# First cross attention: one whole weighting behind the first pair of score steps, and the key and value products of the next chunk in three runs

## The chip, the cores and the metric

The kernel runs on one core of one Trainium2 chip. The metric is the device time of one execution in microseconds, as the median of several runs. The kernel before takes 999.71 us.

## The reference

A two-layer perceiver block: six sublayers update `x` (128 rows of 256 float32 values) one after the other. The change touches only the first of them, a cross attention against 12544 context rows of 256 values:

```python
    def _L0_xattn_ref(input_q, input_k, wq, wk, wv):
        N_HEADS, D_K, D_V_HEAD = 16, 64, 256 // 16
        q = (input_q @ wq).reshape(B, LQ, N_HEADS, D_K).transpose(0, 2, 1, 3)
        k = (input_k @ wk).reshape(B, LK, N_HEADS, D_K).transpose(0, 2, 1, 3)
        v = (input_k @ wv).reshape(B, LK, N_HEADS, D_V_HEAD).transpose(0, 2, 1, 3)
        attn = jnp.einsum('bhqd,bhkd->bhqk', q, k) / jnp.sqrt(jnp.float32(D_K))
        attn = jax.nn.softmax(attn, axis=-1)
        out = jnp.einsum('bhqk,bhkd->bhqd', attn, v)
        ...
    x = x + _L0_xattn_ref(_layernorm(x, axis=-1), ctx_1024, ...)
```

Self attention, a gated feed-forward layer, a second cross attention, a causal self attention and a mixture of 16 experts follow.

## The kernel before

The context is cut into a first chunk of 256 rows (chunk 0, `TAIL_TILES`) and 24 full chunks of 512 rows (chunks 1 to 24). Keys are kept in SBUF per head pair (8 pairs, `m.keys[slot]`), with two slots, one for even and one for odd chunks. PSUM has 8 banks: 0 to 3 hold scores, 4 and 5 the products of keys and values on their way to SBUF, 6 and 7 the output of the weighting.

Every engine has its own program, and the engines meet at semaphores. For one chunk of 512 rows the work is this:

- **Score steps.** There are 8 steps, each for 32 queries and 8 heads. In `scores` (L377) TensorE makes 8 products per step on 64x32 tiles of its array, which the profile shows as 16 matmuls of 512 columns, since each float32 product counts twice. Step t writes banks 0 and 1 or 2 and 3. VectorE takes the maximum (`maxima`, L598), ScalarE two exponentials (`exponentials`, L535) and signals `scores_read`, which frees the banks; VectorE transposes the probabilities (`turn_probabilities`, L617). Step t+2 can only be computed when `scores_read` of step t has come.
- **Key products.** Eight products p = 0 to 7 of the *next* chunk, 6 terms each of 128x128 weights by 512 columns (L354, the context and the weights are split in a high and a low part). ScalarE copies each to SBUF (`keep_keys`, L525) before the bank is used again.
- **Value products.** Two halves of 6 terms each (L361). VectorE transposes them out of PSUM (`turn_values`, L624), and GpSimd sets them aside in a layout with zeros (`set_aside`, L777).
- **Weighting.** `weighted` (L387) multiplies the probabilities of the *previous* chunk by its values: 16 blocks, in the profile 256 matmuls of 128 columns on 64x32 tiles. VectorE transposes the result (`turn_out`, L630), and GpSimd adds it to the sum (`add_out`).
- **Context split.** ScalarE rounds the context of the chunk after next to its high part (`split_context`, L521), and GpSimd subtracts for the low part (L743).

TensorE's order is written out by hand. Before the change `chunk` issues, per chunk, a pair of score steps and something behind it, four times: steps 2 and 3, both value halves of this chunk, the first half of the weighting; steps 4 and 5, keys 0, 1, 2; steps 6 and 7, keys 3, 4, the second half of the weighting; steps 0 and 1 of the next chunk, keys 5, 6, 7. The keys alternate between banks 4 and 5 and the value halves use one each. ScalarE's copies of keys are put between or after exponentials by `KEEP_BETWEEN` and `KEEP_AFTER`. Chunk 1 weights only the 8 blocks of chunk 0. `last_chunk` is a program of its own for chunk 24, with a smaller weighting behind each of its first four steps, and with the two value halves of its own chunk.

SyncE loads the context and issues 16 small DMAs per chunk that place the rescaling factors; GpSimd's `rescale` waits for them.

Of the kernel before, what the change touches and what calls it, by code (L numbers as in the profile page):

```python
# [12 lines left out]
P = 128  # L13
D = 256
DK = D // P
# [5 lines left out]
CHUNK_TILES = 4  # L21
# [6 lines left out]
X0_DV = D // X0_HEADS  # L28
# [319 lines left out]
def xattn0_tensor(pe, m, s, n):  # L348
# [7 lines left out]

    def value_term(slot, half, nt, i):
# [3 lines left out]
        return pe.matmul(m.bank(4 + half)[:, 0:nt * P], w[:, k, half * P:(half + 1) * P], c[:, k, 0:nt * P],  # L361
                         start=(i == 0), stop=(i == TERMS - 1))
# [29 lines left out]

    def values(slot, half, nt):
        pe.wait_ge(s["k_kept"], n("k_kept"))
        for i in range(TERMS):
            done = value_term(slot, half, nt, i)
        done.then_inc(s["v_full"], 1)
# [4 lines left out]

    def next_keys(slot, p, ahead):

        if p < 2:
            values_turned()
        if p == 0:
            pe.wait_ge(s["ctx_split"], n("ctx_split", 2))
            if ahead > 1:
                pe.sem_inc(s["raw_free"], 1)  # L410
        if p >= 2 and p != 5:
            pe.wait_ge(s["k_kept"], n("k_kept"))
        for i in range(TERMS):
            done = key_term(1 - slot, p, CHUNK_TILES, 4 + p % 2, i)
        done.then_inc(s["k_full"], 1)

    def chunk(slot, nt, nt_before, ahead):
        for t in range(0, STEPS, 2):
            if t == FIRST_KEYS:
                pe.wait_ge(s["k_kept"], n("k_kept"))  # L420
            for u in (t, t + 1):
                pe.wait_ge(s["scores_read"], n("scores_read"))
                scores(*step_after(slot, u, nt, ahead, 2))
            for half in VALUES.get(t, ()):
                values(slot, half, nt)
            for p in KEYS_AHEAD.get(t, ()):
                next_keys(slot, p, ahead)
            if nt_before:
                if t == 0:
                    pe.wait_ge(s["probs_turned"], n("probs_turned"))  # L430
                    pe.wait_ge(s["vals_ready"], n("vals_ready"))
                if t in WEIGHT_STEPS:
                    first = 2 * nt_before * WEIGHT_STEPS.index(t)
                    weighted(1 - slot, range(first, first + 2 * nt_before), 4 * nt_before - 1)
                if t == STEPS - 2:
                    pe.wait_ge(s["out_kept"], n("out_kept"))
                    pe.sem_inc(s["out_turned"], 1)

# [8 lines left out]
    def last_chunk(slot, nt, nt_before):  # L447

        for t in range(STEPS):
            after = step_after(slot, t, nt, 0, 2)  # L450
            if after:
                pe.wait_ge(s["scores_read"], n("scores_read"))
                scores(*after)
            if t < 2:
                values(slot, t, nt)
            elif t < 4:
                values_turned()
# [59 lines left out]
def xattn0_scalar(act, m, s, n):  # L517
# [4 lines left out]

    def keep_keys(slot, p, nt):
        act.wait_ge(s["k_full"], n("k_full"))
        act.copy(m.keys[slot][:, p, 0:nt * P], m.bank(4 + p % 2)[:, 0:nt * P]).then_inc(s["k_kept"], 1)  # L525

# [5 lines left out]
    def exponentials(slot, t, nt, between=None):  # L532
        act.wait_ge(s["max_ready"], n("max_ready"))
        for odd in range(2):
            i = act.activation(m.probs[t % 2][:, odd, 0:nt * P], m.ps[:, 2 * (t % 2) + odd, 0:nt * P], ACT.Exp,  # L535
                               bias=m.peak[slot][:, 1, 2 * (t // 4) + odd, t % 4:t % 4 + 1], scale=-1.0,
                               accum_out=m.totals[slot][:, 1, 2 * (t // 4) + odd, t % 4:t % 4 + 1])
            if odd == 0 and between:
                keep_keys(*between, CHUNK_TILES)
        i.then_inc(s["probs_ready"], 1)  # L540
        act.drain().then_inc(s["scores_read"], 1)  # L541

    def chunk(slot, nt, ahead, first=False):
        for t in range(2 if first else 0, STEPS):
# [7 lines left out]
            if kept:  # L552
                for p in KEEP_AFTER.get(t, ()):
                    keep_keys(keys, p, CHUNK_TILES)
            if ahead > 1 and t in SPLIT_STEPS:
                split_context(slot, SPLIT_STEPS.index(t), CHUNK_TILES)

# [6 lines left out]
    for p in range(4):  # L564
        keep_keys(0, p, TAIL_TILES)
    act.wait_ge(s["wk1"], 16)
# [5 lines left out]
    for p in range(4, 6):  # L572
        keep_keys(0, p, TAIL_TILES)
    exponentials(0, 1, TAIL_TILES)
    for p in range(6, 8):
        keep_keys(0, p, TAIL_TILES)
    for k in range(DK):
# [16 lines left out]
def xattn0_vector(dv, m, s, n):  # L594
# [26 lines left out]

    def turn_values(slot, half, nt):
        dv.wait_ge(s["v_full"], n("v_full"))
        dv.transpose(m.vals_t[slot][:, 0:4 * nt, 2 * half:2 * half + 2, :],  # L624
                     m.bank(4 + half)[:, 0:nt * P].rearrange("p (b c d) -> p b c d", c=2, d=X0_DV)
                     ).then_inc(s["v_kept"], 1)
# [6 lines left out]
    def chunk(slot, nt, order, ahead):  # L633
        for t in range(STEPS):
# [9 lines left out]
            turn_probabilities(slot, t, nt)  # L644
            for half in range(2):
                if t == TURN_STEPS[half]:
                    turn_values(slot, half, nt)

    def last_chunk(slot, nt):
        for t in range(STEPS):  # L650
            if t < STEPS - 1:
                maxima(slot, t + 1, nt)
            turn_probabilities(slot, t, nt, (LAST_HALF, STEPS - 1))
            for half in range(2):
                if t == TURN_STEPS[half]:
                    turn_values(slot, half, nt)
            if t == LAST_SUM:
# [82 lines left out]
def xattn0_pool(gp, m, s, n):  # L740
# [40 lines left out]
    def chunk(slot, nt, order, ahead):  # L781
        if order >= 1:
            rescale(1 - slot)
        set_aside(slot, nt)
        if ahead > 1:
            for k in range(DK):
                split_context(slot, k, CHUNK_TILES)
        if order >= 1:
            add_out(1 - slot, "acc_added" if ahead else "acc_whole")

    for k in range(DK):
# [990 lines left out]
```

## Time and profile before

| | us |
|---|---|
| median of 3 runs | 999.71 |
| lowest and highest | 999.46, 1000.55 |
| the profiled execution | 1000.53 |
| its span, first to last instruction | 998.6 |
| mean granted TensorE clock of the span | 0.973 of 2.4 GHz |

The span is 1.93 us shorter than the profiled execution's own time. A row of the timeline view gives the start, the duration, the engine, the line and the operation, how many instructions were merged, and in brackets how long the engine sat idle before and what ended that. PE is the matmul side of TensorE, PEld its loading of weights; a weight load and the matmul that uses it are two rows of the same line.

### The profile page before, as it was taken

What the parts mean: (1) busy time and instruction counts of PE and PEld (TensorE: products, weight loads), DVE (VectorE), ACT (ScalarE), POOL (GpSimd) and SP (SyncE); (2) the same over time, 40 slices, a digit from 0 to 9 for tenths busy, and PEclk for the clock granted to TensorE, in tenths of its full rate; (3) what the DMA queues carried; (4) which work ended last, traced back from release to release, by engine and by line L of the source; (5) the groups of instructions that cost most, each with busy time, mean ns of one, the idle gap of its engine ahead of it and who ended that gap; (6) DMA issues with size and microseconds to landing.
All of it is one profiled execution on the core that took longest, in us unless ns stands there. A gap on an engine that the chain in (4) does not pass through costs nothing.

```text
span 998.6 us, 30527 instructions
## 1 busy us (share of the span) xinstructions
PE 954.4 (96%) x13153; PEld 704.7 (71%) x13153; DVE 690.2 (69%) x871; ACT 588.8 (59%) x1404; POOL 368.8 (37%) x405
## 2 busy tenths in 40 slices
PE   6999999999999999999999999867979998989998
PEld 6666666666666666666666666556967876879998
DVE  3788888888888888888888887831035553357886
ACT  5666666666666666666666666512146662236664
POOL 2354444444444444444444443400023335013332
PEclk9999999999999999999999999986989999789999
DMA  6110000000000000000000000099058888207992
GB/s 217 30 32 15 22 22 24 24 24 24 24 24 24 24 24 24 24 24 24 24 24 24 24 4 3 3 382 358 4 197 268 278 273 305 81 1 256 335 327 101
DMA packets 78294, 97.79 MB, mean 98 GB/s; under 512 B 21584, under 2 KB 56672, under 8 KB 78176
## 3 DMA queue, kind: packets, MB, share of 16 engines
q1 hardware_dynamic: 77088, 94.40, 29.1%
q8 instruction: 103, 1.69, 0.7%
q10 hardware_dynamic: 1088, 1.57, 0.4%
q14 instruction: 15, 0.12, 0.0%
HBM read 95.42 MB, written 0.13 MB: 96 GB/s over the span
## 4 chain that ended last, share of the span: by engine, by line
PE 87%; issue 4%; DVE 3%; POOL 2%; DMA 2%; ACT 1%; SPq 1%; ACTq 0%; DVEq 0%; POOLq 0%
PE ps L354 28%; PE ps L377 17%; PE ps L387 9%; PE ps L361 7%; PE ps L1480 6%; PE ps L1088 3%; PE ps L987 3%; PE ps L1497 2%; PE ps L1501 2%; PE ps L1498 2%; PE ps L1077 1%; PE ps L1079 1%; PE ps L1078 1%; POOL m_w_lo L1463 1%; DMA m_shared_w<-in_m_sw 1%
## 5 line engine op out<-in xcount | busy, mean ns | idle before, releaser
L535 ACT ACTIVATE probs<-ps,x_peak 128x512 f32<-128x512 f32 (+1 forms) x400 | 270.2, 680 | 176.8 <-DVE x_peak L598 166.3
L598 DVE TENSOR_REDUCE x_peak<-ps 128x2 f32<-128x1024 f32 (+1 forms) x200 | 237.0, 1186 | 93.4 <-PE ps L377 93.4
L617 DVE STREAM_TRANSPOSE probsT<-probs 128x1024 f32<-128x1024 f32 (+1 forms) x200 | 242.9, 1215 | 12.9 <-ACT probs L535 12.4
L377 PE MATMUL ps<-keys,qT 64*32 64x512 f32 (+1 forms) x3200 | 195.3, 584 | 2.3 <-ACTq L541 1.6
L354 PE MATMUL ps<-ctxT_hi,wk_hi 128*128 128x512 f32 (+1 forms) x400 | 163.1, 408 | 0.8 <-ACT keys L525 0.8
L354 PE MATMUL ps<-ctxT_lo,wk_hi 128*128 128x512 f32 (+1 forms) x400 | 155.1, 388 | 0.0
L777 POOL TENSOR_SCALAR vals<-vals_t,x_side 128x512 f32<-128x512 f32 (+1 forms) x100 | 152.1, 1538 | 7.4 <-PEq L401 4.5
L354 PE MATMUL ps<-ctxT_hi,wk_lo 128*128 128x512 f32 (+1 forms) x400 | 154.3, 386 | 0.0
L354 PEld LDWEIGHTS ps<-ctxT_hi,wk_hi 128*128 128x128 f32 x400 | 75.5, 189 | 73.6 <-issue 39.8
L525 ACT COPY keys<-ps 128x512 f32<-128x512 f32 (+1 forms) x200 | 110.6, 579 | 28.2 <-PE ps L354 20.3
L743 POOL TENSOR_TENSOR ctxT_lo<-ctx_raw,ctxT_hi 128x512 fp32r<-128x512 f32 x48 | 61.8, 1287 | 135.7 <-ACT ctxT_hi L521 135.7
L377 PEld LDWEIGHTS ps<-keys,qT 64*32 64x32 f32 x3200 | 58.6, 106 | 70.0 <-issue 51.9
L387 PE MATMUL ps<-probsT,vals 64*32 64x128 f32 x6272 | 104.2, 271 | 1.4 <-DVE probsT L617 1.4
L387 PEld LDWEIGHTS ps<-probsT,vals 64*32 64x32 f32 x6272 | 90.5, 105 | 19.7 <-issue 19.5
L354 PEld LDWEIGHTS ps<-ctxT_hi,wk_lo 128*128 128x128 f32 x400 | 75.6, 189 | 15.8
L354 PEld LDWEIGHTS ps<-ctxT_lo,wk_hi 128*128 128x128 f32 x400 | 75.7, 189 | 12.3
L535 ACT ACTIVATION_READ_ACCUMULATOR probs<-ps,x_peak 128x1 f32 x400 | 79.1, 198 | 0.0
L1268 POOL TENSOR_TENSOR c1T_lo<-ctx_two,c1T_hi 128x512 fp32r<-128x512 f32 (+1 forms) x25 | 31.3, 1253 | 105.5 <-ACT c1T_hi L1149 105.5
L760 POOL TENSOR_TENSOR x_parts<-x_totals,x_shrink 128x32 f32<-128x32 f32 x24 | 6.1, 253 | 156.9 <-DMA x_shrinkT<-x_shrink 156.9
L1453 POOL TENSOR_TENSOR m_w_lo<-m_w,m_w_hi 128x1024 fp32r<-128x1024 f32 x15 | 35.5, 2364 | 75.1 <-ACT m_w_hi L1529 75.1
L1480 PE MATMUL ps<-xnT,m_w 128*128 128x128 f32 x512 | 59.9, 275 | 0.0
L1480 PEld LDWEIGHTS ps<-xnT,m_w 128*128 128x128 f32 x512 | 58.6, 192 | 0.3 <-issue 0.3
(250 smaller groups left out, 1307.7 us busy)
## 6 DMA issues: line engine op xcount, KB each, us to landing
m_w<-in_m_w SPq DMA_DIRECT2D x32, 1024.0 KB, 7.7
ctx_raw<-in_ctxT SPq DMA_DIRECT2D x24, 512.0 KB, 3.7
ctx_two<-in_ctxT SPq DMA_DIRECT2D x24, 512.0 KB, 4.0
ctx_one<-in_ctx SPq DMA_DIRECT2D x24, 512.0 KB, 5.0
x_shrinkT<-x_shrink SPq DMA_DIRECT2D x384, 1.0 KB, 1.7
f_h1T<-in_f_h1T SPq DMA_DIRECT2D x1, 4096.0 KB, 18.1
f_h2T<-in_f_h2T SPq DMA_DIRECT2D x1, 4096.0 KB, 27.9
m_shared_w<-in_m_sw SPq DMA_DIRECT2D x2, 1024.0 KB, 7.8
```

Source lines behind the costliest of these rows:

```text
L354: return pe.matmul(m.bank(bank)[:, 0:nt * P], w[:, k, p * P:(p + 1) * P], c[:, k, 0:nt * P], start=(i == 0), stop=(i == TERMS - 1))
L361: return pe.matmul(m.bank(4 + half)[:, 0:nt * P], w[:, k, half * P:(half + 1) * P], c[:, k, 0:nt * P], start=(i == 0), stop=(i == TERMS - 1))
L377: i = pe.matmul(m.ps[32 * j:32 * (j + 1), 2 * (t % 2) + odd, 0:nt * P], m.qT[rows, 4 * group + j, qs], m.keys[slot][rows, 4 * group + j, 0 ...
L387: i = pe.matmul(m.ps[32 * c:32 * (c + 1), 6 + two, 0:P], m.vals[slot][rows, b, c, :], m.probsT[slot][rows, c, b, :], start=(b == 0), stop= ...
L525: act.copy(m.keys[slot][:, p, 0:nt * P], m.bank(4 + p % 2)[:, 0:nt * P]).then_inc(s["k_kept"], 1)
L535: i = act.activation(m.probs[t % 2][:, odd, 0:nt * P], m.ps[:, 2 * (t % 2) + odd, 0:nt * P], ACT.Exp, bias=m.peak[slot][:, 1, 2 * (t // 4) ...
L598: dv.tensor_reduce(m.peak[slot][:, 1, cs, t % 4], m.ps[:, 2 * (t % 2):2 * (t % 2) + 2, 0:nt * P], AX.X, ALU.min).then_inc(s["dve" if t == ...
L617: i = dv.transpose(m.probsT[slot][:, cs, 0:4 * nt, t % 4 * 32:t % 4 * 32 + 32], m.probs[t % 2][:, :, 0:nt * P].rearrange("p c (b k) -> p c ...
L743: gp.tensor_tensor(m.c_lo[slot][:, k, 0:nt * P], m.raw[slot][:, k, 0:nt * P], m.c_hi[slot][:, k, 0:nt * P], ALU.subtract).then_inc(s["ctx_ ...
L777: t = gp.tensor_scalar(m.vals[slot][:, 0:4 * nt, cs, side * X0_DV:(side + 1) * X0_DV], m.vals_t[slot][:, 0:4 * nt, cs, :], m.side[:, side: ...
L1453: eng.tensor_tensor(m.w2_lo[c % 2][:, os, :], second_weights(m, c)[:, os, :], m.w2_hi[c % 2][:, os, :], ALU.subtract).then_inc(s[f"m_w2_lo ...
L1480: t = pe.matmul(m.bank(2 * (c % 2) + half)[:, i * P:(i + 1) * P], w1[:, k, o * P:(o + 1) * P], m.xnT[:, k, :], start=(k == 0), stop=(k == ...
```

## The change

The order of the work on TensorE in `chunk` is new. Behind steps 2 and 3 comes the whole weighting of the previous chunk. Behind steps 4 and 5 come keys 0 and 1 and value half 0 of the next chunk, behind steps 6 and 7 keys 2, 3, 4 and value half 1, behind steps 0 and 1 of the next chunk keys 5, 6, 7. So values are now made one chunk earlier than before, and `last_chunk` and its VectorE part have none left; chunk 0 makes its own values and those of chunk 1. Both value halves go through bank 4, and `KEY_BANKS` gives keys 0, 3, 6 bank 4 and the others bank 5.

The other engines follow: VectorE turns the value halves after steps 4 and 6; ScalarE copies key 2 between the two exponentials of step 6 and splits the context after steps 3 and 5 (before: 5 and 7); VectorE turns the output at step 3 (before: 7); GpSimd's order in a chunk is rescale, split, add the output, split, set the values aside (before: rescale, set aside, two splits, add).

```diff
-VALUES, KEYS_AHEAD = {0: (0, 1)}, {2: (0, 1, 2), 4: (3, 4), 6: (5, 6, 7)}
-WEIGHT_STEPS, FIRST_KEYS = (0, 4), 6
-TURN_STEPS, SPLIT_STEPS, SUM_STEP = (2, 2), (5, 7), 7
-KEEP_BETWEEN, KEEP_AFTER = {0: 5, 4: 0}, {1: (6, 7), 5: (1, 2), 6: (3,), 7: (4,)}
+KEY_BANKS = (4, 5, 5, 4, 5, 5, 4, 5)
+TURN_STEPS, SPLIT_STEPS, SUM_STEP = (4, 6), (3, 5), 3
+KEEP_BETWEEN, KEEP_AFTER = {0: 5, 4: 0, 6: 2}, {1: (6, 7), 5: (1,), 6: (3,), 7: (4,)}
...
     def chunk(slot, nt, nt_before, ahead):
...
+        two_steps(slot, 0, nt, ahead)
+        if nt_before:
+            pe.wait_ge(s["probs_turned"], n("probs_turned"))
+            pe.wait_ge(s["vals_ready"], n("vals_ready"))
+            weighted(1 - slot, range(4 * nt_before), 4 * nt_before - 1)
+            pe.wait_ge(s["k_kept"], n("k_kept", 2))
+        else:
+            for half in range(2):
+                values(slot, half, nt, 4 + half)
+        two_steps(slot, 2, nt, ahead)
+        next_context(ahead)
+        for p in range(2):
+            if not nt_before:
+                values_turned()
+            keys(1 - slot, p, False)
+        values(1 - slot, 0, CHUNK_TILES, 4)
+        if nt_before:
+            pe.wait_ge(s["out_kept"], n("out_kept"))
+            pe.sem_inc(s["out_turned"], 1)
+        two_steps(slot, 4, nt, ahead)
+        keys(1 - slot, 2, True)
+        values_turned()
+        keys(1 - slot, 3, False)
+        keys(1 - slot, 4, True)
+        values(1 - slot, 1, CHUNK_TILES, 4)
+        two_steps(slot, 6, nt, ahead)
+        keys(1 - slot, 5, True)
+        values_turned()
+        keys(1 - slot, 6, False)
+        keys(1 - slot, 7, True)
...
     def last_chunk(slot, nt, nt_before):
...
-            if t < 2:
-                values(slot, t, nt)
-            elif t < 4:
-                values_turned()
+            if t == 1:
+                pe.wait_ge(s["k_kept"], n("k_kept", 2))
...
     def chunk(slot, nt, order, ahead):
         if order >= 1:
             rescale(1 - slot)
-        set_aside(slot, nt)
+        else:
+            set_aside(slot, nt)
         if ahead > 1:
-            for k in range(DK):
-                split_context(slot, k, CHUNK_TILES)
+            split_context(slot, 0, CHUNK_TILES)
         if order >= 1:
             add_out(1 - slot, "acc_added" if ahead else "acc_whole")
+        if ahead > 1:
+            split_context(slot, 1, CHUNK_TILES)
+        if ahead:
+            set_aside(1 - slot, CHUNK_TILES)
```

In the new code `two_steps(slot, t, ...)` waits for `scores_read` and computes step t+2, then does the same for step t+3.

## Rows read from the trace of the kernel before

**Rows 1.** The page: busy time, and the chain that ended last by line

```profile
PE 954.4 (96%) x13153; PEld 704.7 (71%) x13153; DVE 690.2 (69%) x871; ACT 588.8 (59%) x1404; POOL 368.8 (37%) x405
...
PE ps L354 28%; PE ps L377 17%; PE ps L387 9%; PE ps L361 7%; PE ps L1480 6%; PE ps L1088 3%; PE ps L987 3%; PE ps L1497 2%; PE ps L1501 2%; PE ps L1498 2%; PE ps L1077 1%; PE ps L1079 1%; PE ps L1078 1%; POOL m_w_lo L1463 1%; DMA m_shared_w<-in_m_sw 1%
```

**Rows 2.** Windows of one chunk: length, then busy time of each engine, granted clock

```profile
276.39:301.99 25.60, 25.60 (x464) 16.71 (x446) 20.75 (x22) 17.31 (x43) 10.87 (x11) 1.00 0.09 23
```

**Rows 3.** Timeline, matmuls of scores (L377) and weighting (L387), steady chunk

```profile
263.59 1.98 PE L377 MATMUL ps<-keys,qT 64*32 64x512 f32 x32
...
269.80 1.95 PE L377 MATMUL ps<-keys,qT 64*32 64x512 f32 x32
...
274.62 2.03 PE L387 MATMUL ps<-probsT,vals 64*32 64x128 f32 x128
...
276.39 1.98 PE L377 MATMUL ps<-keys,qT 64*32 64x512 f32 x32
```

**Rows 4.** Timeline, weight loads, the same chunk

```profile
265.49 0.19 PEld L354 LDWEIGHTS ps<-ctxT_hi,wk_hi 128*128 128x128 f32 x1 [0.84 <-issue]
...
269.80 0.18 PEld L377 LDWEIGHTS ps<-keys,qT 64*32 64x32 f32 x16 [0.35 <-issue]
...
270.25 0.15 PEld L377 LDWEIGHTS ps<-keys,qT 64*32 64x32 f32 x8 [0.28 <-ACTq L541]
...
271.67 0.19 PEld L361 LDWEIGHTS ps<-ctxT_hi,wv_hi 128*128 128x128 f32 x1 [0.84 <-ACT keys L525]
```

**Rows 5.** Timeline, scores and weighting in the last chunk

```profile
629.36 1.09 PE L377 MATMUL ps<-keys,qT 64*32 64x512 f32 x16
...
636.40 1.12 PE L377 MATMUL ps<-keys,qT 64*32 64x512 f32 x16
...
637.26 1.13 PE L387 MATMUL ps<-probsT,vals 64*32 64x128 f32 x64
...
638.13 1.34 PE L377 MATMUL ps<-keys,qT 64*32 64x512 f32 x12
```

**Rows 6.** Timeline, VectorE behind the pair at 269.80

```profile
270.99 1.23 DVE L598 TENSOR_REDUCE x_peak<-ps 128x2 f32<-128x1024 f32 x1 [1.26 <-PE ps L377]
272.13 1.23 DVE L617 STREAM_TRANSPOSE probsT<-probs 128x1024 f32<-128x1024 f32 x1
273.29 1.19 DVE L598 TENSOR_REDUCE x_peak<-ps 128x2 f32<-128x1024 f32 x1
274.40 1.22 DVE L617 STREAM_TRANSPOSE probsT<-probs 128x1024 f32<-128x1024 f32 x1
```

**Rows 7.** Timeline, ScalarE behind the same pair

```profile
275.77 0.20 ACT L535 ACTIVATION_READ_ACCUMULATOR probs<-ps,x_peak 128x1 f32 x1
...
279.98 0.59 ACT L525 COPY keys<-ps 128x512 f32<-128x512 f32 x1 [0.38 <-PE ps L354]
```

**Rows 8.** Timeline, chunks 0 to 2: first score pairs, and a late fifth step

```profile
22.27 1.09 PE L377 MATMUL ps<-keys,qT 64*32 64x256 f32 x32
...
41.14 1.95 PE L377 MATMUL ps<-keys,qT 64*32 64x512 f32 x32
...
45.96 1.16 PE L387 MATMUL ps<-probsT,vals 64*32 64x128 f32 x64
...
46.85 1.97 PE L377 MATMUL ps<-keys,qT 64*32 64x512 f32 x32
...
47.11 0.20 ACT L535 ACTIVATION_READ_ACCUMULATOR probs<-ps,x_peak 128x1 f32 x1
...
47.40 0.15 PEld L377 LDWEIGHTS ps<-keys,qT 64*32 64x32 f32 x8 [0.34 <-ACTq L541]
...
48.76 0.50 PE L354 MATMUL ps<-ctxT_hi,wk_hi 128*128 128x512 f32 x1
...
65.00 1.95 PE L377 MATMUL ps<-keys,qT 64*32 64x512 f32 x32
```

**Rows 9.** Timeline, one stall of weight loads in chunk 23

```profile
611.26 0.16 PEld L377 LDWEIGHTS ps<-keys,qT 64*32 64x32 f32 x9 [1.00 <-issue]
```

**Rows 10.** Timeline, GpSimd in a steady chunk

```profile
275.74 0.25 POOL L760 TENSOR_TENSOR x_parts<-x_totals,x_shrink 128x32 f32<-128x32 f32 x1 [6.16 <-DMA x_shrinkT<-x_shrink]
...
277.25 6.19 POOL L777 TENSOR_SCALAR vals<-vals_t,x_side 128x512 f32<-128x512 f32 x4 [0.21 <-POOL x_totals L766]
```

**Rows 11.** Timeline, VectorE: the output turned, and a maximum of the last chunk

```profile
289.50 0.45 DVE L630 STREAM_TRANSPOSE out_t<-ps 128x256 f32<-128x256 f32 x1 [0.52 <-PE ps L387]
...
642.60 1.19 DVE L598 TENSOR_REDUCE x_peak<-ps 128x2 f32<-128x1024 f32 x1
```

More of the change, by code:

```diff
@@ L355, in key_term, with value_term @@
                          start=(i == 0), stop=(i == TERMS - 1))
-    def value_term(slot, half, nt, i):
+    def value_term(slot, half, nt, bank, i):
         k, term = divmod(i, 3)
@@ L360, in value_term @@
         c = (m.c_hi, m.c_lo, m.c_hi)[term][slot]
-        return pe.matmul(m.bank(4 + half)[:, 0:nt * P], w[:, k, half * P:(half + 1) * P], c[:, k, 0:nt * P],
+        return pe.matmul(m.bank(bank)[:, 0:nt * P], w[:, k, half * P:(half + 1) * P], c[:, k, 0:nt * P],
                          start=(i == 0), stop=(i == TERMS - 1))
@@ L391, in weighted, with values @@
                 i.then_inc(s[signal], 1)
-    def values(slot, half, nt):
+    def values(slot, half, nt, bank):
         pe.wait_ge(s["k_kept"], n("k_kept"))
         for i in range(TERMS):
-            done = value_term(slot, half, nt, i)
+            done = value_term(slot, half, nt, bank, i)
         done.then_inc(s["v_full"], 1)
@@ L401, in values_turned, with keys @@
         pe.sem_inc(s["vals_turned"], 1)
[L403 to L411 removed]
+    def keys(slot, p, after_keys):
+        if after_keys:
             pe.wait_ge(s["k_kept"], n("k_kept"))
         for i in range(TERMS):
[L414 removed]
+            done = key_term(slot, p, CHUNK_TILES, KEY_BANKS[p], i)
@@ L415, in next_keys, with next_context @@
         done.then_inc(s["k_full"], 1)
-    def chunk(slot, nt, nt_before, ahead):
[L418 to L437, printed above, removed]
+    def next_context(ahead):
+        pe.wait_ge(s["ctx_split"], n("ctx_split", 2))
+        if ahead > 1:
+            pe.sem_inc(s["raw_free"], 1)
@@ new lines, in two_steps @@
+    def two_steps(slot, t, nt, ahead):
+        for u in (t, t + 1):
+            pe.wait_ge(s["scores_read"], n("scores_read"))
+            scores(*step_after(slot, u, nt, ahead, 2))
+    def chunk(slot, nt, nt_before, ahead):
+        two_steps(slot, 0, nt, ahead)
[28 more added lines that the diff above has]
+        keys(1 - slot, 7, True)
@@ L521, in split_context, with keep_keys @@
         act.copy(m.c_hi[slot][:, k, 0:nt * P], m.raw[slot][:, k, 0:nt * P]).then_inc(s["ctx_hi"], 1)
-    def keep_keys(slot, p, nt):
+    def keep_keys(slot, p, nt, bank):
         act.wait_ge(s["k_full"], n("k_full"))
-        act.copy(m.keys[slot][:, p, 0:nt * P], m.bank(4 + p % 2)[:, 0:nt * P]).then_inc(s["k_kept"], 1)
+        act.copy(m.keys[slot][:, p, 0:nt * P], m.bank(bank)[:, 0:nt * P]).then_inc(s["k_kept"], 1)
     def keep_queries(half):
@@ L553, in chunk @@
                 for p in KEEP_AFTER.get(t, ()):
-                    keep_keys(keys, p, CHUNK_TILES)
-            if ahead > 1 and t in SPLIT_STEPS:
-                split_context(slot, SPLIT_STEPS.index(t), CHUNK_TILES)
+                    keep_keys(keys, p, CHUNK_TILES, KEY_BANKS[p])
+            splits = (5, 7) if first else SPLIT_STEPS
+            if ahead > 1 and t in splits:
+                split_context(slot, splits.index(t), CHUNK_TILES)
     for k in range(DK):
@@ L644, in chunk @@
             turn_probabilities(slot, t, nt)
+            if order == 0 and t == 2:
+                for half in range(2):
+                    turn_values(slot, half, nt, 4 + half)
             for half in range(2):
                 if t == TURN_STEPS[half]:
-                    turn_values(slot, half, nt)
+                    turn_values(1 - slot, half, CHUNK_TILES, 4)
     def last_chunk(slot, nt):
```

17 lines of the change are left out of this document (7 added, 10 removed).

## The prediction

> **What bounds the kernel now.** I read the page first. TensorE is busy for 96% of the span, and the chain that ended last runs through its lines: keys, scores, weighting and values make 61% of it [rows 1]. These belong to the first cross attention, so the window view comes next. A steady chunk takes 25.60 us, the matmul row covers all of it, and the clock stays at its upper level, 2.4 GHz [rows 2]. A covered matmul row is no proof that the array works at its pace, so the timeline must say what the 25.60 us are made of. The reader is to see two like halves of 12.80 us in which TensorE is never held up by another engine. The pieces of one half, from start to start: scores behind a weighting 1.90, 18 key terms 4.31, scores behind keys 1.87, 12 value terms 2.95, half a weighting 1.77 [rows 3, 4].
>
> What is waste in these pieces? Six terms are worth 4.31 - 2.95 = 1.36, so 18 are worth 4.08: about 0.2 us go where the array leaves the 128x128 products. One step of scores between 64x32 products takes 0.86 (636.40 to 637.26), a pair 1.72: another 0.15 of the 1.87 go where the keys are entered. From scores to weighting nothing is lost, and 64 weighting matmuls take 0.87 (637.26 to 638.13) [rows 5]. So TensorE can only gain by fewer changes between the two shapes.
>
> What is close behind? The banks of the scores. Let a pair of steps start at time 0, behind keys. VectorE begins its first maximum at 1.19 and its second at 3.49 [rows 6], and the second step's exponentials end at 275.97 - 269.80 = 6.17 [rows 7]. A weight load that waits for this follows 0.09 later (47.11 + 0.20, then 47.40) [rows 8]. So the second step of the *next* pair can't load before 6.26.
>
> **The change on TensorE, steady chunk.** It removes no product. Eight changes of shape per chunk (4 into keys or values, 4 out) become six, and one of the two returns from weighting to scores goes. Let A be the start of the pair of steps 2 and 3.
> - From A to the keys behind steps 4 and 5, by TensorE alone: 1.72 for the pair, 2 x 1.77 = 3.54 for the weighting, 1.90 for the next pair: 7.16.
> - The same by the banks: step 5 is needed at 1.72 + 3.54 + 0.86 = 6.12, but loads at 6.26, streams 0.86 and loses 0.15 into the keys: 7.27. Only here do pairs come closer than before, 5.26 apart instead of 6.21 and 6.59 [rows 3]. The larger value counts, 7.27.
> - From there back to A: 18 terms 4.31, pair 1.87, 24 terms 4.31 + 1.36 = 5.67, pair 1.87, 18 terms 4.31. That is 18.03.
>
> Sum 25.30 against 25.60: 0.30 saved in each of 22 chunks (2 to 23), **-6.6**.
>
> **Why I put no new wait into the 18.03.** The run of keys behind a weighting starts at 265.49 + 12.80 = 278.29; ScalarE copies its first product at 279.98, 1.69 later, for 0.59 [rows 4, 7]. That bank's next user begins 12 terms, 2.7 us, into the run. One product lies between two users of a bank before, and the new bank table keeps that for every key and value inside a run: about 0.4 us to spare. ScalarE must be free in time. Key 2 between the exponentials of step 6 repeats what key 0 does at step 4. Key 3 is ready at 3.05; key 2's copy ended at 2.28 and half an exponential with its read needs some 0.8, so ScalarE is free at about 3.1. Value half 0 is ready as the next pair starts, and VectorE idles 1.26 before that pair's maximum [rows 6]; half 1 likewise, one pair later. Key 3 and key 6, which reuse bank 4 after a value half, come 3 us after the pair's start. The output's transpose of 0.45 [rows 11] falls between the transpose of step 2, over at 5.8, and the maximum of step 4 at 5.26 + 1.2 = 6.4. If that cover went, the maximum would be 0.45 late at most, and the second exponential would still wait for the copy of key 0 first.
>
> **The other queues.** GpSimd gets the same instructions in another order. Rescale waited 6.16 for the small DMAs and began 5.94 behind the pair at 269.80 [rows 10]. SyncE issues those behind the last exponential, which stays about 6.5 before the pair in the new order, and nothing else is queued there but the context load, wanted 20 us later. Behind rescale now stand a split of 1.3, the output, a split and the setting aside (6.19) [rows 10]. VectorE wants the rescaled sums at step 7 and the added output in the next chunk, TensorE the values in the next chunk. All cost 0; the cover is GpSimd's idle time, over half of a chunk (10.87 busy of 25.60) [rows 2]. ScalarE's split after step 3 lies in the 1.4 us before step 4's maximum is ready.
>
> **The ends.**
> - Chunk 0, from 22.27 to 41.14, makes 12 terms of 512 columns more, 2 x 1.36 = **+2.7** [rows 8].
> - Chunk 1 took 65.00 - 41.14 = 23.86 [rows 8]. It has half a weighting and now meets the banks instead: 7.27, and the same 18.03. So 25.30, **+1.4**.
> - Chunk 24 loses its two value halves and is then paced by VectorE: a maximum and a transpose, 2.30 per step (270.99 to 273.29) [rows 6]. Maxima of steps 2 to 5 start at 1.19, 3.5, 5.8, 8.05 behind the first of its steps; one more transpose and the output, and step 6 follows at 10.7. Before it was 642.60 - 629.36 = 13.24 [rows 5, 11]. **-2.6**, and the chain behind it is the same, with the weight loads of the next layers, which are triggered by it.
>
> Sum: -6.6 + 2.7 + 1.4 - 2.6 = -5.1. Against the profiled execution's own time of 1000.53 (1.93 more than its span, which stays) this is 995.4. The median of the runs shown is 0.82 lower, 999.71, so I forecast **994.6**.
>
> **What no row shows.** A full-rate weighting of 256 matmuls in one run doesn't occur. From below it costs 3.41, four times the 0.853 that 64 take in pure streaming (0.86 for a step is the same work). From above I take 3.54 plus the largest stall of TensorE's own feed in these chunks, 1.00 of "issue" in chunk 23 [rows 9], so 4.54. 64 took 0.89 (45.96 to 46.85) and 128 took 1.77 [rows 3, 8]: the second 64 were no slower than the first, and I stay with 3.54. The lower end would change nothing, since the banks bind.
>
> The Trainium skill has a rule about the gain: TensorEngine Tiling (Array Packing), section Key Properties, says that changing the tiling mode drains the array, while changing the tile does not. By it only the count of changes matters, and the sum would hold 7.16 where I have 7.27, which is the first rival. About the feed, Runtime: NRT & Kernel Launch, section Instruction fetch mechanics, says that code is fetched in blocks of 256 instructions and that crossing a block is mostly hidden; it speaks against the second rival, and the stall in the row shows that mostly is not always.
>
> **Rivals.**
> 1. *The banks don't bind*, because a late load is hidden. The chunk is 25.19, 0.41 saved: -9.0, with the ends -7.5, so **992.2**. For it: in chunk 1 the second step's load waited 0.34 for ScalarE, and the keys still came 1.91 behind the pair, as ever [rows 8]. Against it: that load came 0.55 into the pair, before its need at 0.86; the new one is 0.14 past it. Chance 0.15.
> 2. *The long weighting outruns its feed* (slower). The ends and chunk 1 sum to +1.5, so a chunk that saves under 0.07 makes the kernel slower. That is so once the 256 matmuls take 0.34 more than 3.54 (0.11 of it hides behind the banks). At 1.00 more: (1.00 - 0.41) x 22 = +13.0, so **1014**; at half of that 0.09 x 22 = +2.0, so 1003. For it: the one stall stands right behind a weighting. Against it: no steady chunk has one. Chance 0.14.
> 3. *Half of the gain goes into a new wait*: a copy or a turned value late by 0.2 per chunk where I count 0.4 or less to spare. +4.4, so **999.0**, no change that can be told. Chance 0.17.
>
> My forecast keeps 0.52, with its own range of 993 to 997; the other 0.02 are for things not thought of. 0.2%, 2 us, is about what a measurement of this kernel can tell from no change. Faster: forecast and first rival, 0.68. Same: third rival, 0.18. Slower: 0.14. The range leaves out the most of the second rival and a tail below the first: 991.5 to 1001.
>
> **What would show it.** Steady chunks of 25.30. Keys 7.27 behind the pair of steps 2 and 3, and the load of step 5 at 6.26 with a wait for ScalarE (rival 1: keys at 7.16). A weighting of 3.5 (rival 2: longer, or "issue" in or behind it). No wait of the second to fourth product of a run (rival 3). In chunk 24 step 6's maximum at 10.7. Wrong would be any wait of TensorE for VectorE's turned values, or of VectorE for GpSimd.

## The result, and the profile after

The changed kernel takes 1035.78 us (median of 4 runs, 1027.94 to 1038.28), the kernel before on the same chip 999.59 (4 runs, 998.26 to 1000.55). The ratio is 1.0358 with an interval of 1.0323 to 1.0394: the change costs 36 us. The profiled execution took 1033.98 with a span of 1032.0.

The page of the changed kernel, its busy times and its chain by engine, beside [rows 1]; the last row is the chain by engine of the kernel before:

```profile
PE 957.3 (93%) x13153; PEld 705.5 (68%) x13153; DVE 697.9 (68%) x871; ACT 589.8 (57%) x1404; POOL 368.3 (36%) x405
...
PE 85%; issue 7%; DVE 4%; POOL 2%; DMA 1%; ACT 1%; SPq 1%; ACTq 0%; DVEq 0%; POOLq 0%
...
PE 87%; issue 4%; DVE 3%; POOL 2%; DMA 2%; ACT 1%; SPq 1%; ACTq 0%; DVEq 0%; POOLq 0%
```

The counts are the same, 13153 matmuls and as many loads, and TensorE's busy time grew by only 3 us. No work was added; 33 us (1032.0 - 998.6) of span came as idle time. "issue", time in which an engine waited for nothing that the profile shows, is 7% of the chain where it was 4%. The view of waits from 66 to 640 us says where (total, times, longest):

```profile
PEld ps L376 <- issue: 70.7, 196, 2.1
...
PEld ps L386 <- issue: 36.2, 63, 2.1
...
PE ps L386 <- issue: 18.6, 18, 1.8
PE ps L376 <- issue: 8.6, 10, 1.6
```

The same view of the kernel before has for the first two:

```profile
PEld ps L377 <- issue: 48.5, 176, 1.0
...
PEld ps L387 <- issue: 16.7, 47, 0.5
```

The last two rows of the changed kernel, 27.2 us together, have no counterpart before. There TensorE's matmul row had no wait for issue at all in these 574 us, and its weight loads none above 1.0. Both are at the scores (L376) and the weighting (L386). Two steady chunks in the window view, beside [rows 2] (length, then busy time of each engine, granted clock, share and rate of the DMAs):

```profile
259.63:287.44 27.81, 26.49 (x445) 16.81 (x445) 21.01 (x21) 17.37 (x44) 11.49 (x13) 1.00 0.09 22
287.44:314.26 26.82, 25.52 (x445) 16.94 (x445) 21.02 (x21) 17.37 (x44) 11.50 (x13) 1.00 0.09 22
```

They take 27.81 and 26.82 us, where I forecast 25.30 and the chunk before took 25.60. The clock is at its upper level, 2.4 GHz, in both, so it isn't the clock. The timeline of the matmuls between the pair of steps 2 and 3 and the keys, in the first of them and then the second:

```profile
259.63 1.95 PE L376 MATMUL ps<-keys,qT 64*32 64x512 f32 x32
261.37 2.16 PE L386 MATMUL ps<-probsT,vals 64*32 64x128 f32 x136
263.94 1.85 PE L386 MATMUL ps<-probsT,vals 64*32 64x128 f32 x116 [0.41 <-issue]
...
267.56 1.92 PE L376 MATMUL ps<-keys,qT 64*32 64x512 f32 x25 [0.91 <-issue]
269.42 0.50 PE L353 MATMUL ps<-ctxT_hi,wk_hi 128*128 128x512 f32 x1
...
287.44 1.95 PE L376 MATMUL ps<-keys,qT 64*32 64x512 f32 x32
289.18 3.03 PE L386 MATMUL ps<-probsT,vals 64*32 64x128 f32 x201
293.51 0.97 PE L386 MATMUL ps<-probsT,vals 64*32 64x128 f32 x52 [1.30 <-issue]
...
294.42 1.89 PE L376 MATMUL ps<-keys,qT 64*32 64x512 f32 x27
296.24 0.50 PE L353 MATMUL ps<-ctxT_hi,wk_hi 128*128 128x512 f32 x1
```

The reader is to see a group of matmuls broken off, 0.41 to 1.30 us in which nothing is issued, and the rest of the same group. It breaks in the weighting (after 136 matmuls, after 201) and in the scores behind it (after 7 of 32). The keys come 9.79 and 8.80 behind the start of the pair, where the forecast has 7.27. The breaks are longer for the weight loads, which run ahead: 1.81 at 267.56.

In the rest of the chunk nothing is off: from the keys to the next pair, 269.42 to 287.44, it takes 18.02 (forecast 18.03). None of the waits that I had named as a sign of error is there: no wait of TensorE for VectorE's turned values or for a copy between products, none of VectorE for GpSimd.

Chunk 1 is the exception that shows the forecast chunk. Two weight loads behind its first pair:

```profile
49.64 0.18 PEld L376 LDWEIGHTS ps<-keys,qT 64*32 64x32 f32 x16 [1.55 <-ACTq L553]
50.66 0.19 PEld L353 LDWEIGHTS ps<-ctxT_hi,wk_hi 128*128 128x128 f32 x1 [0.84 <-issue]
```

It has half a weighting (128 matmuls). Its pair starts at 43.39, step 5's load waits for ScalarE until 49.64, 6.25 behind it (forecast 6.26), and the keys come at 50.66, 7.27 behind (forecast 7.27).

### The profile page after: what moved, and what is told of

Its sections match the earlier page's. It is cut to its first block, busy times and chain, and to the rows that moved or that the text cites. A ratio compares the mean times of both kernels' runs of the same rounds, so it can differ in the third digit from the quotient of the medians.

```text
span 1032.0 us, 30526 instructions
## 1 busy us (share of the span) xinstructions
PE 957.3 (93%) x13153; PEld 705.5 (68%) x13153; DVE 697.9 (68%) x871; ACT 589.8 (57%) x1404; POOL 368.3 (36%) x405
## 3 DMA queue, kind: packets, MB, share of 16 engines
q8 instruction: 103, 1.69, 0.7%
## 4 chain that ended last, share of the span: by engine, by line
PE 85%; issue 7%; DVE 4%; POOL 2%; DMA 1%; ACT 1%; SPq 1%; ACTq 0%; DVEq 0%; POOLq 0%
PE ps L353 27%; PE ps L376 18%; PE ps L386 9%; PE ps L360 6%; PE ps L1497 6%; PE ps L1105 3%; PE ps L1004 3%; PE ps L1514 2%; PE ps L1518 2%; PE ps L1515 2%; PE ps L1094 1%; DVE x_peak L611 1%; DVE probsT L630 1%; PE ps L1095 1%; POOL m_w_lo L1480 1%
## 5 line engine op out<-in xcount | busy, mean ns | idle before, releaser
L376 PE MATMUL ps<-keys,qT 64*32 64x512 f32 (+1 forms) x3200 | 203.4, 586 | 13.2 <-issue 8.9
L537 ACT COPY keys<-ps 128x512 f32<-128x512 f32 (+1 forms) x200 | 112.9, 577 | 38.2 <-PE ps L353 30.3
L386 PEld LDWEIGHTS ps<-probsT,vals 64*32 64x32 f32 x6272 | 94.8, 105 | 42.5 <-issue 42.5
L386 PE MATMUL ps<-probsT,vals 64*32 64x128 f32 x6272 | 104.2, 270 | 21.1 <-issue 19.3
L376 PEld LDWEIGHTS ps<-keys,qT 64*32 64x32 f32 x3200 | 53.8, 106 | 99.6 <-issue 79.4
L637 DVE STREAM_TRANSPOSE vals_t<-ps 128x512 f32<-128x512 f32 (+1 forms) x50 | 35.2, 705 | 36.1 <-PE ps L360 36.1
```

The lines of the kernel that those rows point to most:

```text
L376: i = pe.matmul(m.ps[32 * j:32 * (j + 1), 2 * (t % 2) + odd, 0:nt * P], m.qT[rows, 4 * group + j, qs], m.keys[slot][rows, 4 * group + j, 0 ...
L386: i = pe.matmul(m.ps[32 * c:32 * (c + 1), 6 + two, 0:P], m.vals[slot][rows, b, c, :], m.probsT[slot][rows, c, b, :], start=(b == 0), stop= ...
L537: act.copy(m.keys[slot][:, p, 0:nt * P], m.bank(bank)[:, 0:nt * P]).then_inc(s["k_kept"], 1)
```

## The experiments

Each kernel's own pace is read as two numbers: the time from the start of the pair of steps 2 and 3 to the keys behind it (the *stretch*), and from one such pair to the next (the *chunk*). Matmuls are counted as the trace does, which shows one fp32 matmul of the code as two, each with a weight load beside it. So the whole weighting is 256 matmuls or 512 instructions, and between two runs of 128x128 products stand 32 + 256 + 32 = 320 matmuls, 640 instructions.

**Half the weighting.** The changed kernel with blocks 8 to 15 of the weighting left out, 384 instructions in the stretch.

```diff
-            weighted(1 - slot, range(4 * nt_before), 4 * nt_before - 1)
+            weighted(1 - slot, range(2 * nt_before), 2 * nt_before - 1)
```

> The changed kernel with the second half of each chunk's weighting left out (8 of 16 blocks, so 128 matmuls in one run instead of 256; the output of the first attention loses the other half). Theory 1, the instruction feed: a run of 64x32 matmuls with 128 columns uses up instructions faster than they are fetched, and only a run longer than about one fetched block stalls. Then no stall of 'issue' is left; the keys come 7.27 us behind the pair of steps 2 and 3, held by ScalarE's exponentials, a steady chunk is 25.3 us and the kernel takes about 990 to 995 us, though only 1.77 us of matmuls per chunk went. Theory 2, the new order has a wait that was not counted (copies, turned values, GpSimd): the stall stays, the distance falls by about 1.8 us at most, to 7.4 or more, and stalls remain elsewhere in the chunk. Theory 3, the 256 matmuls are just slow, in proportion: the distance is held by the banks too, 7.27, so the second run must tell it from theory 1.

Measured: 991.81 us (4 runs), ratio 0.9907 to the kernel before (0.9882 to 0.9932). Every stretch from chunk 2 on takes 7.27 to 7.29 and every chunk 25.30. So the new order does all that it was said to do, its shape changes, its banks, the other three queues, once the weighting is short. One thing was expected and isn't so: breaks with "issue" are not all gone. The largest, in the chunk from 373.44 on:

```profile
378.40 0.14 PEld L376 LDWEIGHTS ps<-keys,qT 64*32 64x32 f32 x3 [0.70 <-issue]
```

It costs nothing, since step 5 behind it must wait for its bank anyway: TensorE by itself would need 5.39 of the 7.27.

**Half the instructions, the same work for the array.** Each matmul of the weighting streams 256 columns (two blocks) in place of 128, with the weights of every second block. The array streams the same number of columns; the weights of every second block aren't loaded, and the output isn't the reference's.

```diff
-        for b in blocks:
+        for b in range(0, blocks, 2):
...
-                    i = pe.matmul(m.ps[32 * c:32 * (c + 1), 6 + two, 0:P], m.vals[slot][rows, b, c, :],
-                                  m.probsT[slot][rows, c, b, :], start=(b == 0), stop=(b == last),
+                    i = pe.matmul(m.ps[32 * c:32 * (c + 1), 6 + two, 0:2 * P], m.vals[slot][rows, b, c, :],
+                                  m.probsT[slot][rows, c, b:b + 2, :].rearrange("p b q -> p (b q)"),
+                                  start=(b == 0), stop=(b == blocks - 2),
```

> The changed kernel with each weighting matmul two blocks wide: 256 columns instead of 128, half as many instructions, the same number of columns streamed through the same tiles (the weights of every second block are not used, so the first attention's output is changed). Theory 1, the instruction feed: 256 instructions instead of 512 in the run, no stall, the weighting takes about 3.45 us, the keys come 7.27 us behind the pair of steps 2 and 3, a steady chunk is 25.3 us, the kernel about 990 to 995 us. Theory 3, the array, its operands' reads or its clock make a long run slow: the columns are the same, so the distance stays at 8.5 to 10.8 us and the kernel near 1035. Theory 2, an uncounted wait: likewise near 1035.

Measured: 992.99 us (5 runs), ratio 0.9917 (0.9883 to 0.9952). Stretch 7.27 to 7.28, chunk 25.30. Its timeline:

```profile
296.69 1.95 PE L376 MATMUL ps<-keys,qT 64*32 64x512 f32 x32
298.44 3.66 PE L396 MATMUL ps<-probsT,vals 64*32 64x256 f32 x128
301.89 2.15 PE L376 MATMUL ps<-keys,qT 64*32 64x512 f32 x32
```

The weighting takes 301.89 - 298.44 = 3.45, unbroken. This settles the main question. The columns streamed and the order of all engines are those of the changed kernel; only the instructions are half as many, matmuls and weight loads alike, and the loss is gone whole.

**The whole weighting in one run, in the old order.** The kernel before, with its weighting not in two halves but behind the values of steps 0 and 1. Between two runs of 128x128 products stand 256 + 32 matmuls, 576 instructions.

```diff
-                if t in WEIGHT_STEPS:
-                    first = 2 * nt_before * WEIGHT_STEPS.index(t)
-                    weighted(1 - slot, range(first, first + 2 * nt_before), 4 * nt_before - 1)
+                if t == 0:
+                    weighted(1 - slot, range(4 * nt_before), 4 * nt_before - 1)
```

> The kernel before with one part of the change alone: both halves of the weighting in one run behind steps 2 and 3 and the value products, everything else in the old order. Without a feed limit: one pair of steps now comes 4.8 us behind the other (between keys 3 and 4), so the banks hold it about 0.6 us, a steady chunk of 26.2 us, the kernel 1013 us. With theory 1, the instruction feed: on top of it the stall that the changed kernel has, about 1.5 to 1.9 us per chunk, in the middle of the weighting, 'issue' as its cause: 27.7 to 28.1 us per chunk, the kernel 1045 to 1054 us. If the stall came from another part of the change (values a chunk early, banks, the split), it would be absent here.

Measured: 1047.3 us (one run). Its timeline from one such weighting to the next:

```profile
264.09 3.78 PE L387 MATMUL ps<-probsT,vals 64*32 64x128 f32 x256
267.60 1.05 PE L377 MATMUL ps<-keys,qT 64*32 64x512 f32 x8
269.02 1.92 PE L377 MATMUL ps<-keys,qT 64*32 64x512 f32 x24 [0.37 <-issue]
275.18 1.95 PE L377 MATMUL ps<-keys,qT 64*32 64x512 f32 x32
280.00 1.09 PE L377 MATMUL ps<-keys,qT 64*32 64x512 f32 x16
281.49 1.09 PE L377 MATMUL ps<-keys,qT 64*32 64x512 f32 x16 [0.40 <-ACTq L540]
...
291.66 3.06 PE L387 MATMUL ps<-probsT,vals 64*32 64x128 f32 x201
296.09 0.97 PE L387 MATMUL ps<-probsT,vals 64*32 64x128 f32 x52 [1.38 <-issue]
```

The same breaks, 0.37 and 1.38, in another place of another order. A chunk takes (652.21 - 70.51) / 21 = 27.70, inside what theory 1 expected; part of its loss has another cause, a bank that is late by 0.40 for the pair at 280.00. So the long run alone brings the stalls, and the new order of the keys and values isn't needed for them.

**Three quarters.** As the first, with 12 of 16 blocks: 384 instructions in the run, 512 in the stretch.

> The changed kernel with 12 of 16 blocks of the weighting (192 matmuls in one run; the last quarter is left out). Theory 1, the instruction feed: 384 instructions in the run and 512 in the stretch between two runs of keys; most chunks still stall, but shorter, the distance from the pair of steps 2 and 3 to the keys between 7.27 and 9 us, on average about 7.8, the kernel about 1003 us. A slowness in proportion to the run's length would give a third less than the 1.9 us lost per chunk, so about 8.5 and 1022 us.

Measured: 994.89 us (one run). The expectation of some stalls is missed. Not one stretch stalls:

```profile
295.96 1.95 PE L376 MATMUL ps<-keys,qT 64*32 64x512 f32 x32
297.71 2.88 PE L386 MATMUL ps<-probsT,vals 64*32 64x128 f32 x192
...
302.22 1.09 PE L376 MATMUL ps<-keys,qT 64*32 64x512 f32 x16 [0.78 <-ACTq L553]
```

The last row's wait is the bank's, which was in the forecast: step 5 starts 302.22 - 295.96 = 6.26 behind its pair. So the loss doesn't grow evenly with the weighting's length. Two things make this run milder than its length alone: TensorE by itself would need 6.28 here, so the bank would hide a break of up to 0.99; and the blocks in which instructions arrive end at nearly the same place in every chunk of this run (see where the breaks stand, below).

**Fourteen blocks.** 448 instructions in the run, 576 in the stretch.

> The changed kernel with 14 of 16 blocks of the weighting (224 matmuls in one run, 448 instructions; the last two blocks are left out). 12 blocks had no stall and 16 blocks lost 1.94 us per chunk. Theory 1 with a store of instructions that is used up: the stall sets in between, so some chunks stall by up to 1.5 us and others not; 26.0 us per chunk on average, about 1010 us. A slowness in proportion to the length is already excluded.

Measured: 1014.85 us (one run). Stretches of 7.48 to 9.12; the chunks from 67.95 to 622.01 take 554.06 / 21 = 26.38, 1.08 above 25.30. With 512 instructions the loss is nothing, with 576 it is 1.08, with 640 it is 1.94, each as an average over its chunks.

**Twelve blocks, then four.** The whole work again, but broken up: 12 blocks, step 4, 4 blocks, step 5. If the unbroken run of the weighting were what counts, this would stay near the run with three quarters.

```diff
-            weighted(1 - slot, range(4 * nt_before), 4 * nt_before - 1)
+            first = 12 * nt_before // 4
+            weighted(1 - slot, range(first), 4 * nt_before - 1)
             pe.wait_ge(s["k_kept"], n("k_kept", 2))
+            pe.wait_ge(s["scores_read"], n("scores_read"))
+            scores(*step_after(slot, 2, nt, ahead, 2))
+            weighted(1 - slot, range(first, 4 * nt_before), 4 * nt_before - 1)
+            pe.wait_ge(s["scores_read"], n("scores_read"))
+            scores(*step_after(slot, 3, nt, ahead, 2))
...
-        two_steps(slot, 2, nt, ahead)
```

> The changed kernel, all work done, with the weighting cut in two inside the same stretch: 12 blocks behind the pair of steps 2 and 3, then step 4, then the last 4 blocks, then step 5. No change of tile shape is added, and step 5 can't load before 6.26 us anyway. Theory 1, the instruction feed: the stretch still holds 640 instructions, but 512 of them are due by 5.3 us instead of 576, and the other 128 come at 5.3 to 6.3 us. If one more fetched block has come by then, the stall is gone, the keys come 7.27 us behind the pair, 25.3 us per chunk and 988 to 995 us in all, faster than both kernels. If only the number of instructions between two runs of keys counted, the stall would stay near 1.9 us per chunk and the kernel near 1035 us.

Measured: 1031.77 us (4 runs), ratio 1.0324 (1.026 to 1.0388), so nearly all of the loss stays. The chunks take (637.86 - 69.29) / 21 = 27.07. One of them:

```profile
260.14 3.19 PE L386 MATMUL ps<-probsT,vals 64*32 64x128 f32 x188
263.26 1.05 PE L376 MATMUL ps<-keys,qT 64*32 64x512 f32 x12
264.00 1.07 PE L386 MATMUL ps<-probsT,vals 64*32 64x128 f32 x55
266.29 0.32 PE L386 MATMUL ps<-probsT,vals 64*32 64x128 f32 x5 [1.22 <-issue]
```

The break of 1.22 has moved to the end of the second part. A step of scores between the parts (16 matmuls in 0.86 us, in which the weighting would issue 62) gives the feed almost nothing. The stretch has 640 instructions here as there, and where they stand in it changes little.

**The weighting twice.** The changed kernel computes each weighting twice over (1024 instructions in one run), to see the pace at which TensorE is fed when nothing else limits it.

```diff
+            weighted(1 - slot, range(4 * nt_before), 4 * nt_before - 1, signal=None)
             weighted(1 - slot, range(4 * nt_before), 4 * nt_before - 1)
```

> The disputed cost by itself: the changed kernel with the whole weighting computed twice in one run (512 matmuls, 1024 instructions; the second pass overwrites the first, the result is the same). The array needs 3.5 us more. Theory 1: behind the first 400 or so instructions the pace is that of the feed, one block of 256 instructions per 3.7 us or so instead of per 1.77, so the added 512 instructions take about 7.5 us: the distance from the pair to the keys rises from about 9.2 to 16 to 17 us, and the kernel takes about 1190 us. A fixed stall of one late fetch per run would give 9.2 + 3.5 = 12.7 us, and 1112 us.

Measured: 1200.42 us (one run), stretches of 15.69 to 18.25 from chunk 2 on, on average (803.84 - 70.90) / 21 - 18.03 = 16.87. Part of its timeline:

```profile
318.00 2.16 PE L386 MATMUL ps<-probsT,vals 64*32 64x128 f32 x136
320.79 2.03 PE L386 MATMUL ps<-probsT,vals 64*32 64x128 f32 x128 [0.63 <-issue]
324.52 2.03 PE L386 MATMUL ps<-probsT,vals 64*32 64x128 f32 x128 [1.70 <-issue]
328.25 1.85 PE L386 MATMUL ps<-probsT,vals 64*32 64x128 f32 x116 [1.70 <-issue]
```

And, of windows of 0.25 us in the same stretch (columns as above, the rate last), two in which the DMAs moved over 40 GB/s:

```profile
325.50:325.75 0.25, 0.25 (x38) 0.25 (x31) 0.00 (x0) 0.00 (x0) 0.00 (x0) 1.00 0.29 66
329.25:329.50 0.25, 0.25 (x38) 0.25 (x30) 0.00 (x0) 0.00 (x0) 0.00 (x0) 1.00 0.34 66
```

66 GB/s for 0.25 us is 16.5 KB, every 3.75 us. The groups are exactly 128 matmuls, which with their loads are 256 instructions, here every 3.73 us (320.79, 324.52, 328.25), of which 2.03 is work and 1.70 is idle. Over all 52 places of this run where two breaks follow each other one block apart, it is 3.34 to 4.03 us, 3.70 on average. The pages bear it out: this row counts the packets of the instruction queue, first before, then here:

```profile
q8 instruction: 103, 1.69, 0.7%
...
q8 instruction: 148, 2.42, 0.9%
```

The trace has 11520 records of TensorE more than the changed kernel's, which has the same 103 packets as before, and 11520 / 256 = 45. One packet of 16.4 KB is one block of 256 instructions.

**The same instructions, shifted.** The kernel before, with 128 waits that are already met put ahead of TensorE's first work. The trace records 64 waits for them, 0.11 us apart, so later instructions lie 64 places further, and not the 128 that were meant. If stalls belong to a place in the code relative to the blocks, the one of [rows 9] should move.

```diff
     pe.wait_ge(s["ident"], 1)
+    for _ in range(128):
+        pe.wait_ge(s["ident"], 1)
```

> The kernel before with 128 waits that are already met put ahead of TensorE's first work, so that every later instruction lies 128 places further in TensorE's code. Theory 1: the one stall of 1.00 us of the kernel before, in chunk 23, is a block boundary at a bad place; it moves to another place or goes, and steady chunks stay at 25.60, since their longest stretch between two runs of keys has 384 instructions, under what 12 blocks (512) passed without a stall. The time stays within 2 us of 999.6, apart from what the waits themselves take at the start. If the alignment of blocks decided alone, chunks would now stall.

Measured: 997.17 us (one run; the kernel before on that chip took 992.42 to 1001.54, so the total says nothing). The stall of 1.00 in the first half of chunk 23 is gone, and steady chunks stay at 25.60. In its place the second half of chunk 23 has one, behind the same 23 weight loads of the score pair as in [rows 9]:

```profile
625.33 0.16 PEld L377 LDWEIGHTS ps<-keys,qT 64*32 64x32 f32 x9 [0.61 <-issue]
```

It costs 0.68 us (4.36 from the half weighting to the keys, where others take 3.68; [rows 9] cost 1.07). In the last chunk a group of the weighting waits too, 1.63 at its loads, where it waited 0.49 before; that one I can't place. The move by half a chunk is what the shift asks for. Half a chunk is 447 records of TensorE, and 447 + 64 = 511 is two blocks of 256, to within one. So [rows 9] was no accident of its chunk but the same thing, at a place set by where the blocks end.

## Why the prediction was wrong

**The step that failed is the one under "What no row shows": "64 took 0.89 and 128 took 1.77: the second 64 were no slower than the first, and I stay with 3.54."** Two lengths of at most 128 matmuls are at most one block of 256 instructions; they can't show what comes when a second block is wanted 1.77 us after the first, while blocks come about 3.7 us apart. The weighting of 256 matmuls, with the score pair behind it, cost 1.94 a chunk more than I had.

The sum against the measurement, in the profiled executions:

- Steady chunks 2 to 23 took 668.05 - 68.71 = 599.34, 27.24 each, against 25.30 forecast: 42.7 us more.
- Before they took (629.36 - 65.00) / 22 = 25.65 by [rows 5, 8], not 25.60; the 0.05 a chunk is -1.1 that I had left out. Nearly all of it is the one stall of [rows 9].
- Chunk 0 took 43.39 - 21.82 = 21.57 against 18.87: +2.70 (forecast +2.7). Chunk 1 took 25.32: +1.46 (forecast +1.4).
- Chunk 24's maximum of step 6 starts 678.65 - 668.05 = 10.60 behind its first step (forecast 10.7, before 13.24): -2.64.
- From chunk 24's start to the end of the span it is 363.95 against 369.24. Of these 5.29 us, 2.64 are the last term; 2.65 more came off in the layers behind, which I had at nothing. Of these, 1.8 lie in one piece of work, from the first matmul of L1351 to the first of L1359 (L1368 and L1376 after): 7.90 us before at a granted clock of 0.54, 6.10 after at 0.72. The rest isn't explained; nor are 0.45 us at the start.

995.4 + 42.7 - 1.1 - 2.65 - 0.45 = 1033.9, and the profiled execution took 1033.98. The other steps of the sum held. The stretch is bound by the scores' banks at 7.27, not at TensorE's own 7.16: the stretch is 7.27 to 7.29 with half, three quarters and the wide weighting alike, though TensorE by itself would need 5.39, 6.28 and 7.07 there (7.16 less what their weighting saves of 3.54). That rejects the first rival. The 18.03, the ends, and "no new wait" for copies, turned values and GpSimd held as well, which rejects the third.

**The second rival was the right one, and I gave it 0.14.** It named the mechanism and its place ("outruns its feed", "issue in or behind it") and the sign. Its time, 1003 to 1014, is too low by half the loss or more, because its price of 1.00 came from a single stall of the old order; the new one has up to two breaks in a chunk, of up to 2.1 us at the weight loads. Measured against TensorE's own 7.16, the stretch takes 9.21 on average, 2.05 more.

**What could have been read before.** The page's DMA rows say that instructions come as 103 packets in 1.69 MB, 16.4 KB each, and TensorE has 2 x 13153 = 26306 records [rows 1]. That is 255 records in a packet, so practically all packets are TensorE's. In the trace before they start 3.5 to 12 us apart in the steady chunks; those at 269.04, 276.33 and 283.71, for one, are 7.3 and 7.4 apart. Half a weighting uses up 256 instructions in 1.77 us [rows 3]. A supply of which no two blocks stood less than 3.5 us apart was asked for two blocks in 3.54 us, and my "from above" of one stall was no bound. I had read the Trainium skill here, Runtime: NRT & Kernel Launch, section Instruction fetch mechanics, which says that code comes in blocks of 256 instructions and that crossing one is mostly hidden. The runs agree with the block of 256; of "mostly hidden" they show the limit, since in this order the crossings cost 1.94 us a chunk.

**Where the breaks stand.** The number of weight loads that TensorE had issued just before three breaks of the changed kernel, those that end at 263.94, 267.56 and 293.51 (window, busy time, count, then clock, DMA share and rate):

```profile
0.00:263.90 263.90, 162.54 (x3906) 1.00 0.14 41
0.00:267.50 267.50, 164.35 (x4034) 1.00 0.14 40
0.00:293.50 293.50, 180.23 (x4415) 1.00 0.14 39
```

They are 128 and 381 loads apart. With the matmuls and the waits recorded between them that is 257 and 767 records, one and three blocks of 256 to within one. It is so everywhere. TensorE's program lays all chunks out one behind the other, without a loop. I counted all its records in order, loads, matmuls and waits, and took every "issue" of over 0.6 us before a weight load of scores or weighting (the regular ones of every chunk are under it), between the start of chunk 2 and the last chunk. There are 29 in the changed kernel, 22 with fourteen blocks, 30 with twelve and four, 74 with the doubled weighting, 23 in the old order with the whole weighting, one each in the kernel before, the shifted one and the one with half the weighting, none with three quarters or the wide weighting. All 181 stand at record 193 or 194 above a multiple of 256. A break is TensorE at the end of a block, with the next one not there.

This also says why long and short chunks alternate (27.32, 27.80, 26.86, 27.77, 26.61, 27.67, ...). A chunk has 894 records, so two chunks are 1788 and seven blocks 1792. In the chunk at 259.63 blocks end 81, 337 and 593 records behind the pair, and it breaks at the last two; in the chunk at 287.44 they end at 211 and 467, and it breaks once. With each further two chunks the ends move by 4 records. In the kernel before they move likewise: blocks end 5 and 261 records into the half weighting of chunk 3 and 41 and 297 in chunk 21, without a break, and at 45 and 301 in chunk 23 comes [rows 9]. With three quarters a chunk has 766 records, nearly three blocks, and they end at 3 to 45 and at 259 to 301 in every chunk. So that run shows 512 instructions without a break at this one place only. With fourteen blocks the place changes from chunk to chunk, and the stretch with it, from 7.48 to 9.12.

**How the feed makes the breaks.** The windows in which a block lands, in the chunks at 259.63 and 287.44:

```profile
261.00:261.25 0.25, 0.25 (x16) 0.10 (x8) 0.25 (x1) 0.03 (x1) 0.00 (x0) 1.00 0.35 66
...
265.00:265.25 0.25, 0.25 (x38) 0.25 (x22) 0.25 (x1) 0.25 (x3) 0.03 (x1) 1.00 0.27 66
...
291.00:291.25 0.25, 0.25 (x37) 0.25 (x31) 0.25 (x2) 0.25 (x2) 0.00 (x0) 1.00 0.27 66
...
294.50:294.75 0.25, 0.25 (x13) 0.07 (x6) 0.10 (x1) 0.00 (x0) 0.25 (x1) 1.00 0.29 66
```

A break ends 2.2 to 2.9 us after a packet has started (261.0 to 263.94, 265.0 to 267.56, 291.0 to 293.51; so in all 29), and the next packet starts about 1.1 us after work resumes (265.0, 294.5). The two add up to some 3.7, the pace of the doubled weighting. That is a reading of where the bursts lie: what happens between a block's transfer and its use, no row shows. The pace itself is shown. In the slow parts the engine issues 36 instructions in 4.31 us for 18 terms, far more slowly than blocks come, so the feed catches up there. How far it can run ahead stays open, and so does what sets single values, as the 10.81 at 368.31.

**A version that keeps the gain?** With 12 blocks in the stretch it is 25.30, but the other four must stand elsewhere and cost half of 1.77, which the stretch, bound by the banks, doesn't give back: 25.30 + 0.89 = 26.19, above the 25.60 of before. Other cuts put back a change between the two shapes. None was run; that none wins is argued from these numbers, not shown.

## What to carry to other kernels

Count instructions, not only the array's time. In this kernel TensorE was fed 256 instructions per 3.7 us when it waited for them, about 14.5 ns each, and the small-tile fp32 weighting used one each 6.9 ns (1.77 us for 256). Such a group runs at full speed only on what has been fetched ahead, and slow instructions (128x128 products of 512 columns, 0.23 us each) give the feed time for that. So before merging two runs of short matmuls to save changes of shape, add up the instructions between the slow runs on either side. Here 640 cost 1.94 us and 576 cost 1.08 on average, against the 0.30 that the merge saved; 512 cost nothing, at the one place of the block ends that was run and with 0.99 us of slack. It is no fixed threshold: single breaks of up to 1.00 stand in stretches of under 400. If such a run must be long, make its matmuls wider: the same columns in half the instructions cost nothing.

A price for something that no row shows isn't bounded by rows of a shorter run. Where "issue" appears even once behind a dense group, ask what supplies the instructions and how far apart its transfers stand before doubling that group.

## What the runs showed of the hardware

- TensorE's instructions arrive in blocks of 16.4 KB that hold 256 of them (45 packets more for 11520 records more), and where it waits for them, one block every 3.34 to 4.03 us, 3.70 on average; its small matmuls use one up in 1.77 to 2.03.
- The breaks stand at the ends of these blocks: 181 of 181 over 0.6 us, in eight kernels, at the same place above a multiple of 256 records.
- Where the ends of blocks fall decides what a stretch loses: 0.2 to 1.9 us with 576 instructions. With two chunks near seven blocks, long and short chunks alternate.
- Changing between 128x128 products and 64x32 products costs what the rows before gave: 7.27 and 18.03 held to 0.02 in every run in which the feed kept up.
- 64 recorded waits, put ahead of all work, moved a stall from the first half of chunk 23 to the second, 447 records later.
